# Decoder kernel: landmark scores from 32-row blocks, no wide POOL passes, Newton results of the crossed pairs left in the other half

## The reference

```
block 1 (n)   Nystrom self attention, 16 heads of 8, 64 landmarks (means of 2 positions):
              k1 = softmax(Q Kl'), k2 = softmax(Ql Kl'), k3 = softmax(Ql K')
              V = inverse of k2 by 6 steps  V = 0.25 V (13 I - KV (15 I - KV (7 I - KV)))
              out = ((k1 V) (k3 v)) w_proj
block 2 (r1)  cross attention to ctx, 16 heads of 8, a relative bias per head
block 3 (rm)  8 experts with a hidden width of 256, the best one per position
block 4 (r2)  causal self attention, 16 heads of 8
block 5 (ry)  masked cross attention with its own layer norms, 16 heads of 64
block 6 (rf)  FFN whose two weights are mixed from 32 low-rank factors (softmax of logits),
              gelu between them
```

## Time and profile before

| | |
|---|---|
| median of 3 runs | 2525.32 us |
| profiled execution's own time | 2522.18 us |
| its span, first to last instruction | 2520.2 us |
| mean granted TensorE clock | 0.953 |
| TensorE, VectorE, ScalarE, POOL busy | 2266.3, 1956.9, 1450.1, 387.1 us |
| DMA | 35.75 MB, mean 14 GB/s |

### The profile page before, as it was taken

The page is one execution under the profiler, slowest core; times in us unless marked ns, Lnnn a source line. Parts: engine busy times, 40 slices in busy tenths (PEclk is TensorE's granted clock), DMA queues, the critical chain, the costliest instruction groups (busy, mean ns, idle before and its releaser), DMA issues.

```text
span 2520.2 us, 95538 instructions
## 1 busy us (share of the span) xinstructions
PE 2266.3 (90%) x40576; PEld 1846.1 (73%) x40576; DVE 1956.9 (78%) x6166; ACT 1450.1 (58%) x5093; POOL 387.1 (15%) x530
## 2 busy tenths in 40 slices
PE   6789999999999999999999999999999999999875
PEld 3677777777777777777777777777777777777764
DVE  3568888888888888788888888788888888888652
ACT  3346666656656655656656565665656566566531
POOL 2101111111111111111111111111111111111110
PEclk9889999999999999999999999999999999999885
DMA  4200000000000000000000000000000000000000
GB/s 192 90 7 9 5 7 9 9 9 9 9 5 7 9 9 8 9 5 8 8 9 9 9 9 5 8 8 9 9 9 9 5 7 9 9 9 8 6 3 2
DMA packets 29960, 35.75 MB, mean 14 GB/s; under 512 B 3544, under 2 KB 28128, under 8 KB 28384
## 3 DMA queue, kind: packets, MB, share of 16 engines
q1 hardware_dynamic: 29536, 29.65, 3.4%
HBM read 27.54 MB, written 2.10 MB: 12 GB/s over the span
## 4 chain that ended last, share of the span: by engine, by line
PE 52%; DVE 28%; ACT 15%; issue 4%; POOL 0%; DMA 0%; SPq 0%; POOLq 0%; DVEq 0%; ACTq 0%
PE ps L477 29%; PE ps L480 8%; ACT probs L1062 5%; PE ps L744 4%; DVE probsT L1349 3%; PE ps L828 3%; ACT probs L1047 3%; PE ps L876 2%; ACT ey L985 2%; DVE x_rows L1211 2%; DVE small L1252 2%; PE ps L761 2%; PE ps L665 2%; DVE qk_v L1337 1%; DVE p L1254 1%
## 5 line engine op out<-in xcount | busy, mean ns | idle before, releaser
L1102 POOL TENSOR_TENSOR small<-small,weights 128x1 f32<-128x1 f32 x256 | 149.0, 582 | 1142.7 <-DVE small L1200 1142.7
L1010 ACT ACTIVATE probs<-ps,small 128x128 f32<-128x128 f32 x1024 | 286.1, 384 | 31.0 <-DVE small L1342 29.5
L1349 DVE COPY probsT<-ps 128x512 f32<-128x512 f32 x384 | 263.1, 685 | 36.3 <-PE ps L480 32.7
L480 PE MATMUL ps<-weights,probs 128*128 128x128 f32 x1536 | 256.1, 292 | 32.8 <-ACT probs L1010 15.4
L1342 DVE TENSOR_REDUCE small<-ps 128x4 f32<-128x512 f32 x384 | 254.2, 683 | 20.5 <-PE ps L828 10.7
L1113 POOL TENSOR_TENSOR probs<-probs,small 128x256 f32<-128x256 f32 x128 | 108.7, 849 | 885.6 <-DVE small L1478 885.6
L480 PEld LDWEIGHTS ps<-weights,probs 128*128 128x128 f32 x1536 | 178.7, 146 | 86.3 <-ACT probs L1010 44.6
L929 ACT COPY x_T<-ps 128x128 f32<-128x128 f32 x128 | 34.1, 267 | 302.9 <-PE ps L480 302.9
L1062 ACT ACTIVATE probs<-ps,small 128x128 f32<-128x128 f32 x512 | 181.6, 375 | 20.5 <-DVE small L1342 19.0
L477 PE MATMUL ps<-wz,ss 64*64 64x72 f32 x6144 | 157.4, 229 | 32.5 <-DVE wz L1294 32.4
L1293 DVE SCALAR_TENSOR_TENSOR wz<-ey,ss 128x256 f32<-128x256 f32 x320 | 142.0, 444 | 51.1 <-ACT ss L970 36.9
(11 more groups left out here) (199 smaller groups left out, 5400.0 us busy)
## 6 DMA issues: line engine op xcount, KB each, us to landing
weights<-in_wpack SPq DMA_DIRECT2D x3, 1759.0 KB
fc_A<-in_b SPq DMA_DIRECT2D x2, 2048.0 KB, 14.3
fc_A<-in_a SPq DMA_DIRECT2D x2, 2048.0 KB, 11.4
x_in_T<-in_xT SPq DMA_DIRECT2D x32, 64.0 KB, 1.8
x_in_rows<-in_x SPq DMA_DIRECT2D x32, 64.0 KB, 1.8
ctx_T<-in_ctxT SPq DMA_DIRECT2D x32, 64.0 KB, 1.9
ctx_rows<-in_ctx SPq DMA_DIRECT2D x32, 64.0 KB, 1.9
mask_i<-in_mask SPq DMA_DIRECT2D x32, 64.0 KB, 1.9
```

What stands on the lines that cost most here:

```text
L480: return nc.tensor.transpose(dst, src, ident)
L1010: ins = nc.scalar.activation(probs(s, g)[:, j], bank(s, SCORE_BANK[g], 128 * j, 128), ACT.Exp, bias=sm(s, "nb", 4 * g + j, 1), scale=-1.0)
L1102: nc.gpsimd.tensor_tensor(sm(s, out), sm(s, ve), w("mhalf"), ALU.pow).then_inc(sem(done, s), 1)
L1349: V.tensor_copy(probsT(s, n % 4).rearrange("p a b -> p (a b)"), bank(s, 2)).then_inc(sem("pT", s), 1)
```

## The change

POOL has no masks and no scalings any more: VectorE does the whole softmax scaling. The landmarks are masked in one pass with a mask of 4 columns (`half4`) per 32-row block, and the score products contract over the 32 rows of a block, two row blocks in turn. The first four score steps become two (n.a0, n.a1); the second waits for all exponentials of the first. kk is one step that alternates between the row halves. S results of group 1 stay in the other half: ScalarE copies all 128 partitions at once, and VectorE's sums are made per half, with inputs from different halves. W's group 1 result comes back to its own half by a second crossing. The last W and n.w are crossed as well. The factors of the second FFN weight have their own buffers and are loaded right behind the weights; the small factors are scaled in quarters; f1's matmuls are cut into two of 256 columns. The first projection no longer waits for the rows of x. All places are new (`PERIOD` 74.45336 to 74.74847).

```diff
@@ pe, nystrom
-            for t in range(4):
-                b = (t + 1) % 2
...
-                for c in range(2):
-                    h = TJ * t + 2 * c
-                    mm = one(bank(s, b, 192 * c, 192), qlm[:, h:h + 2].rearrange("p a b -> p (a b)"), k1[:])
+            for half in range(2):
...
+                else:
+                    pe.wait_ge(sem("n_exp", s), at("n_exp", s, 2))
                 for c in range(2):
+                    for t in (2 * half, 2 * half + 1):
+                        mm = one(bank(s, (t + 1) % 2, 192 * c, 192),
+                                 qlm[quarters[t], 2 * c:2 * c + 2].rearrange("p a b -> p (a b)"), k1[quarters[t]])
...
+                    g = 2 * i + half
+                    one(bank(s, 1 - half, 256 * i, 256), q1[quarters[g]], klm[quarters[g]].rearrange("p a b -> p (a b)")
...
-            for c in range(2):
-                pe.wait_ge(sem("n_eT", s), at("n_eT", s, 3 + c))
-                for i in range(4):
+            pe.wait_ge(sem("n_eT", s), at("n_eT", s, 4))
+            for i in range(4):
+                for c in range(2):
...
-                            mm = one(PS[s][halves[m if last else m ^ g], g, PW * i + a:PW * i + PW], ss[halves[m], p, 0:M],
+                            mm = one(PS[s][halves[m ^ g], g, PW * i + a:PW * i + PW], ss[halves[m], p, 0:M],
...
-            for h in range(H):
-                _, _, p, m = heads(h)
-                mm = one(PS[s][m, 0, 16 * p:16 * p + HD], p2[m, p], ey[m, p, M:PW])
+            for i in range(4):
+                for g in range(2):
+                    p = 4 * g + i
+                    for m in range(2):
+                        mm = one(PS[s][halves[m ^ g], g, 16 * i:16 * i + HD], p2[halves[m], p], ey[halves[m], p, M:PW])
@@ act, nystrom (the 0.25 copies L985 likewise)
-                for m in range(2):
-                    ins = copy(ss[halves[m], ps], src[halves[1 - m]])
-                ins.then_inc(sem("newton_act", s), 1)
+                copy(ss[:, ps], src).then_inc(sem("newton_act", s), 1)
@@ dve, nystrom
-                V.tensor_tensor(alone[:, 0:H // 2], every(dst, H // 2), over(w("mask16", 0, H // 2), M), ALU.mult
-                                ).then_inc(sem("n_lm", s), 1)
+                V.tensor_tensor(alone[:], every(dst, TJ), over(w("half4"), M), ALU.mult).then_inc(sem("n_lm", s), 1)
...
-                    Ey, Y = ss[:, ps, M:PW], ey[:, ps, M:PW]
+                    places = ((slice(0, 128),) * 2,) if g == 0 else tuple(zip(halves, halves[::-1]))
                     if k < NEWTON - 1:
-                        V.scalar_tensor_tensor(wz[:, ps, 0:M], ey[:, ps, 0:M], 3.0, ss[:, ps, 0:M], ALU.mult, ALU.add)
-                    V.scalar_tensor_tensor(wz[:, ps, M:PW], Y, 4.0, Ey, ALU.mult, ALU.add).then_inc(sem("newton_dve", s), 1)
-                    V.tensor_tensor(uy[:, ps], Ey, Y, ALU.add).then_inc(sem("newton_u", s), 1)
+                        for there, here in places:
+                            V.scalar_tensor_tensor(wz[there, ps, 0:M], ey[here, ps, 0:M], 3.0, ss[there, ps, 0:M], ALU.mult, ALU.add)
+                    for there, here in places:
+                        ins = V.scalar_tensor_tensor(wz[there, ps, M:PW], ey[here, ps, M:PW], 4.0, ss[there, ps, M:PW],
+                                                     ALU.mult, ALU.add)
+                    ins.then_inc(sem("newton_dve", s), 1)
+                    for there, here in places:
+                        ins = V.tensor_tensor(uy[here, ps], ss[there, ps, M:PW], ey[here, ps, M:PW], ALU.add)
+                    ins.then_inc(sem("newton_u", s), 1)
...
+            for g in range(2):
+                v = bank(s, g, 0, 64).rearrange("p (a b) -> p a b", b=16)[:, :, 0:HD]
+                for m, half in enumerate(halves):
+                    ins = V.tensor_tensor(w9[half, 4 * g:4 * g + 4, m, 0:HD], v[halves[m ^ g]],
+                                          sm(s, "rd", 4 * g, 4)[half].unsqueeze(2).to_broadcast([M, 4, HD]), ALU.mult)
@@ dve, y_scale (POOL's y_scale and its half of n.lm0, n.lm1 are deleted)
-                v = probs(s, g)[:, 2:4]
-                V.tensor_tensor(v, v, over(r[:, 2:4], 128), ALU.mult).then_inc(sem("y_p", s), 1)
+                V.tensor_tensor(probs(s, g), probs(s, g), over(r, 128), ALU.mult).then_inc(sem("y_p", s), 1)
@@ sp, start
-            sp.wait_ge(once("composed"), 1)
             factor_loads(1)
@@ pool, start
-                nc.gpsimd.tensor_tensor(small, small, over(mix_col[:, n], D), ALU.mult).then_inc(once("scaled"), 1)
+                for q in range(4):
+                    part_of = mixed[n][0][:, 4 * q:4 * q + 4]
+                    nc.gpsimd.tensor_tensor(part_of, part_of, over(mix_col[:, n, 4 * q:4 * q + 4], D), ALU.mult
+                                            ).then_inc(once("scaled"), 1)
```

144 lines of the change are left out of this document (62 added, 82 removed), and 102 rows, old and new, of tables (PLACES, START).

## The result

The changed kernel takes 2582.57 us (median of 4 runs, 2574.51 to 2585.37), the kernel before 2521.66 in the same set: ratio 1.0232, interval 1.0205 to 1.0259. I had forecast 2497, faster, with a range up to 2575; the kernel came out slower, and its time lies above the range.

A forecast was written before the change was run, and what follows sets the result against it. The prediction took the Nyström stream's path through one batch, a chain over several engines, as the period. Its terms summed to -0.75 us per batch, -23 over 31, with -5 at the start: 2497 us, 8-in-10 range 2435 to 2575.

The forecast's parts named there:

- front "-0.84 -0.61 -0.53": Before the Newton steps, VectorE's landmark sum of k, row step and masks get shorter, all on the chain: -1.98 us per batch.
- Newton S and W halves, queue (+0.68, -0.80, +1.5): Five Newton iterations: S halves longer by split sums, W halves shorter by full copies, work queued behind VectorE's sums.
- scalings: y softmax scaling done whole on VectorE, four instructions of +0.25 us, three on the chain: +0.75 us per batch.
- last iteration: copy, sums, product: Sixth Newton iteration: copy -0.40 us, sums 0.53 to 0.48, product in four quadrants -0.40.
- w product, w passes, order at the end: Behind the last iteration: w product -0.40 us, four w passes for two +0.35; order moves together zero.
- strings: Six split Newton sums in a row on VectorE, between copy and product, each held: 1.66 us instead of 0.55.
- "2 of 5 bare": Newton halves: no other TensorE work covers the change in 2 of 5 iterations: S +0.68 us, W -0.80 per batch.
- "together zero within 0.5 us": New order on every engine, including VectorE's moved layer-norm step and last y scaling: no net effect within 0.5 us.
- "VectorE becomes the bound": Rival: Newton products wait for VectorE's queue, +1.9 us per batch, 2579 us as median; 32% together with the clock.
- "Nothing moves": Rival: front and end are won, the middle lost, -0.75 becomes 0, only the start gains: 2520 us; 18%.
- "full relief": Rival: TensorE's and ScalarE's savings come through, -3.3 us per batch, 2415 to 2420 us; 13%.
- The clock: Rival: less busy TensorE gets full clock less often, +40 to +59 us in all; within the slower chance of 32%.

The follow-up runs named there:

- e1: Changed kernel with the Newton part of the kernel before (half-partition copies, unsplit sums, last product in two quadrants): 2529.5 us, 1.0022 of the kernel before.
- e2: Kernel before with only the Newton edit (full copies, sums split over both halves, crossed last product), old order: 2649.2 us, 1.0511.
- f1: Changed kernel with half-partition copies and unsplit sums, and half of each y scaling on POOL again: 2550.3 us, 1.0132 of the kernel before.
- j6: Kernel before with POOL's two wide landmark passes cut from 128x512 to 128x8 after the first batch: 2493.7 us, 0.9903.
- i1: Changed kernel with half-partition copies and unsplit sums, but the change's form in the last Newton iteration: 2546.4 us, 1.0095 of the kernel before.
- l2: Changed kernel without its Newton edit, three steps at the end of the period moved in the order: 2514.4 us, 0.9968 of the kernel before.
- e3: Changed kernel with full copies but group 1's sums unsplit, leaving out the crossing's correction: 2460.0 us, 0.9765 of the kernel before.
- k1: Changed kernel without any crossing in the Newton products, all copies full, all sums whole: 2610.2 us, 1.0368 of the kernel before.
- e8: Kernel before with only the change's front (landmark masks on VectorE, 32-row scores), old order: 2671.5 us, 1.0606.
- f2: Changed kernel with half-partition copies and unsplit sums, in the order of the kernel before: 2660.3 us, 1.0558 of the kernel before.
- e5: Changed kernel with six sums for group 1, each with inputs and output in one half, crossing left out: 2528.3 us, 1.0040 of the kernel before.
- e6: Changed kernel with the six crossed sums ordered by half instead of by kind: 2576.0 us, 1.0216 of the kernel before.

## Why the prediction was wrong

By the steps of the sum, us per clean period:

| step as predicted | predicted | measured | from |
|---|---|---|---|
| front "-0.84 -0.61 -0.53" | -1.98 | -0.75 | first windows |
| Newton S and W halves, queue (+0.68, -0.80, +1.5) | +1.38 | +1.48 | middle windows, change against e1 |
| scalings | +0.75 | +0.68 with the order | middle windows, e1 against before |
| last iteration: copy, sums, product | -0.85 | +0.10 | third and fourth windows, change against e1 |
| w product, w passes, order at the end | -0.05 | +0.60 | third and fourth windows, e1 against before |
| sum | -0.75 | +2.11 | |

**The middle was right in sum, partly by luck.** Its rise, +2.16, is what I had (+2.13). The strings' price (1.66) and VectorE's total (66.4 forecast, 65.3 measured) held, and so did the net of split and copies in this order; in the old order the same edit lengthens the five iterations by 2.75 (e2, medians of clean periods). Its parts were less good: "2 of 5 bare" is contradicted by the chain, which holds most of the strings, and the 1.5 us by VectorE's 28% share made up for it. The scalings' entry is a coincidence as far as I can show: with half of them back on POOL (f1) the period did not shorten. What lengthens the middle by 0.68 in the new order stays open.

**The front step failed, by 1.23 us, the largest error.** I added up three savings on one engine as if each arrived in full. The landmark sum and the masks put VectorE 1.38 us ahead at the end of the masks (1.59 us after q for 2.97), but it then waits for TensorE, 0.48 and 0.19 us, and is 0.52 ahead at the first row minimum and 0.35 at the row step. j6, with the long masks, is as far at the first row minimum (3.77 and 3.76): the masks' 0.53 brought nothing there, and at most 0.12 at the end of the front (27.20 to 27.08, two orders apart). The row step is 0.34 us in the changed kernel, but VectorE waits 0.40 behind it for matmuls. And the 32-row scores have the wait that I had priced at "0 to 0.8 us; I take 0": TensorE's idle time for the exponentials ahead of the scores is 13.9 + 10.3 us, 0.76 a batch, where it was 1.9 + 1.2. The matmuls were 126 and 196 ns, not 110 and 146.

**The last-iteration step failed too, by 0.95 us.** "Copy -0.40, product -0.40" took every shortening as bare. i1 gives them 0.06 together: in TensorE's order the product's successor is another stream's, and waits for VectorE instead. **So did the order**, "together zero within 0.5 us": e1, with no Newton edit, has +0.60 in the last two windows, of which the end behind w is +0.76, and l2 takes away 0.64 of it by moving three steps.

**The start** gained nothing: I had -5 us; q to the fourth q takes 5.6 more and the rest from the last q 2.1 less.

**The rivals.** "VectorE becomes the bound" gave 2579, near the 2582.6, but its ground is not shown. VectorE is at 65.3 of 74.8 us; relieving ScalarE by 5.67 us and TensorE by 0.6, with VectorE as it was (e1 to e3), still shortens the period by 2.13, and adding to TensorE alone (e3 to k1) lengthens it by 4.89. Its own sign, Newton products waiting for VectorE in most iterations, came in part: more than 0.5 us ahead of 52 of 160 W products. The runs fit a Newton loop that is one serial chain over three engines, with none of them alone the bound; that no engine is it near TensorE's 92% isn't shown. Its price was near by luck: it paid +4.8 for strings, scalings and queue, where the middle rose by 2.16, and took the front and the last iteration at -2.88, where with the order they gave -0.05. "Nothing moves" and "full relief" are out by the measured time. The clock was not the cause in the changed kernel, but it was nearer than I gave it credit for: with the same front in the other order it falls in every period (e8) or nearly every one (f2).

## What to carry to other kernels

In a mesh of streams with the order written out, price an edit by taking it out and by adding as much at its place. One microsecond was worth 0.92 of period when added to the Newton products (4.89/5.30), 0.62 in VectorE's sums (3.70/5.99), and 0.36 in ScalarE's copies (1.87/5.20, middle windows of e1 and e3). In the front it was worth about 1 when added (0.81/0.74) and half when taken away (0.63/1.26). No share of a chain gives these. Savings that lie in a row on one chain don't add: after the first, look at what else the next instruction in order waits for. And when an edit comes with a new order, measure the order's ends first: here it kept the clock (f2 is 5% above e1) and cost 0.64 us a period in a place where three steps could be moved back.

## What the runs showed of the hardware that I had not expected

- Two SBUF inputs in different halves of the partitions hold a VectorE instruction until the one ahead has ended, whatever the order: 0.19 to 0.21 us between starts of 64x32 sums, 0.10 with both inputs in one half (e5, e6).
- The granted clock can fall at the same place of every period: in e8 to 1.2 GHz for 13.7 us, about 7.3 us after q, in 28 periods of 28. TensorE was busy for 4.50 of the 7.30 us before it; in the changed kernel it was busy for 5.69, and the clock did not fall there.
- Matmuls of 64 rows by 64 columns and 72 wide cost 38.2 ns each in two quadrants (k1) and 24 in four (148.3/6144 in the changed kernel). Leaving the crossing out costs 3.4 to 3.7%, more than, in the new order, half copies (0.2%) or split sums (2.3%); in the old order the split sums cost more (5.1%, e2).
- POOL's scaling of 128x256 takes 0.85 us where VectorE's takes 0.43, and of the 1.07 us that it takes over VectorE gains 0.24 (f1).
- Beside POOL's wide pass VectorE's 128x64 sum takes 1.06 us, and 0.22 once the pass is cut to 128x8 (j6).
